# Edge softmax in steps of 512 columns, with the forward maxima of a backward step kept in PSUM

## The reference

```
h = relu(layernorm(x)); x = x + segment_sum((h * W)[src], dst)                    # layer 0
h = relu(layernorm(x)); x = x + sage(relu(sage(h)))                               # layer 1, two mean aggregations
h = relu(layernorm(x)); x = x + attention(h, edge_attr)                           # layer 2
h = relu(layernorm(x)); x = x + segment_sum(h[src] @ W.T + b, dst) / deg          # layer 3

attention: eh = edge_attr @ W_fcr.T                        # 212,500 x 64
           m  = segment_max(eh, dst);  ex = exp(eh - m[dst])
           agg = segment_sum(ex / segment_sum(ex)[dst] * ((h @ W_fc.T)[src] + eh), dst)
           h_new = relu(where(deg > 0, agg + h @ loop_W, h))
```

## Time and profile before

| stretch | us | what runs |
|---|---|---|
| 0 to 388 | 388 | keys sorted, first norm, first 64 pieces cleared; the scatter begins at 251.7 |
| 388 to 746 | 358 | forward softmax steps; scatter goes on; DMA share 0.99 |
| 746 to 905 | 159 | backward steps alone, last pieces cleared; DMA share 1.01 |
| 905 to 2462 | 1557 | backward steps with chunks 0 to 640 |
| 2462 to 2590 | 128 | last 60 chunks; the scatter ends at 2553 |
| 2590 to 6919 | 4329 | rest of layer 0, layers 1 to 3 |
| profiled execution | 6921.18 | span 6919.3, granted TensorE clock 0.913 |

### The profile page before, as it was taken

How to read it: one execution, slowest core, us unless ns; L and a number is a source line. 1 busy time by engine, 2 the same in 40 slices (tenths; PEclk the granted TensorE clock), 3 DMA queues, 4 the chain that set the end, 5 groups by cost and what they waited for, 6 DMA issues and landing times.

```text
span 6919.3 us, 127730 instructions
## 1 busy us (share of the span) xinstructions
PE 5262.2 (76%) x47666; PEld 4799.9 (69%) x47667; DVE 4606.4 (67%) x6014; ACT 3720.1 (54%) x2906; POOL 3433.8 (50%) x3412
## 2 busy tenths in 40 slices
PE   0057478888888753999999999855888888788886
PEld 0023267777777653999999999855777777677776
DVE  9757567777777658788877888733555555555554
ACT  0100167666666543788777777600555454454565
POOL 0457777777777750000000000077777777777730
PEclk9988789999999886999999999977999999999998
DMA  9999977666666545666666666533777677676785
GB/s 344 351 273 297 335 234 215 209 214 210 212 214 215 175 117 141 181 195 194 191 189 186 195 196 197 161 80 90 158 151 159 153 156 154 140 155 148 157 143 110
DMA packets 1628347, 1313.89 MB, mean 190 GB/s; under 512 B 911250, under 2 KB 1528211, under 8 KB 1627311
## 3 DMA queue, kind: packets, MB, share of 16 engines
q1 hardware_dynamic: 840725, 948.43, 46.1%
q10 hardware_dynamic: 674448, 299.80, 18.4%
q0 software_dynamic: 112592, 57.76, 5.1%
HBM read 833.34 MB, written 311.54 MB: 165 GB/s over the span
## 4 chain that ended last, share of the span: by engine, by line
PE 40%; DVE 7%; ACT 5%; issue 4%; DMA 3%; POOL 3%; DVEq 1%; SPq 0%; ACTq 0%; POOLq 0%
PE pair L1650 22%; PE pair L1769 8%; PE wide L1793 7%; ACT u L1542 3%; POOL u L1151 3%; ACT batch L1542 1%; PE wide L1832 1%; DVE u L918 1%; DMA extra<-hi_b,tsel 1%; DMA u<-zrows,stage 1%; DVEq L415 1%; DVE batch L983 1%; DMA u<-cells 1%; PE flip L1750 0%; DVE u L616 0%
## 5 line engine op out<-in xcount | busy, mean ns | idle before, releaser
L1650 PE MATMUL pair<-tab,u 128*128 128x192 bf16 (+1 forms) x29106 | 2579.5, 249 | 184.9 <-ACT u L1400 179.7
L1650 PEld LDWEIGHTS pair<-tab,u 128*128 128x128 bf16 x29106 | 2503.9, 99 | 213.3 <-ACT u L1400 183.3
L1400 ACT ACTIVATE u<-u 128x1792 bf16<-128x1792 uint8 (+1 forms) x1360 | 2269.6, 1703 | 608.4 <-PE pair L1650 347.4
L1151 POOL DMA_INDIRECT u<-zrows,stage x1664 | 1613.7, 970 | 1318.2 <-DMA zrows<-batch 782.6
L616 DVE TENSOR_REDUCE u<-u 128x1792 bf16<-128x1792 uint8 (+1 forms) x838 | 1675.1, 2021 | 662.9 <-PE pair L1650 508.4
L1116 POOL DMA_INDIRECT cells<-val,idx x1664 | 1727.9, 1038 | 755.2 <-issue 741.7
L1769 PE MATMUL pair<-u 128*128 x4880 | 939.3, 350 | 405.7 <-DVE u L918 388.9
L1769 PEld LDWEIGHTS pair<-u 128*128 128x128 f32 x4880 | 855.8, 204 | 481.6 <-issue 480.3
L1542 ACT ACTIVATE u<-u 128x1792 bf16<-128x1792 uint8 x317 | 524.7, 1684 | 320.8 <-PE wide L1793 313.1
L1609 PE MATMUL wide<-u,wbd 128*128 128x512 f32 (+1 forms) x1120 | 508.9, 588 | 179.4 <-DMA u<-in_ea 108.2
L1632 PE MATMUL flip<-ident,u 128*128 128x128 f32 x840 | 264.7, 329 | 382.9 <-DVE u L752 370.4
(11 more groups left out here) (270 smaller groups left out, 4337.4 us busy)
## 6 DMA issues: line engine op xcount, KB each, us to landing
u<-cells SPq DMA_DIRECT2D x2100, 224.0 KB, 3.1
cells<-zt SPq DMA_DIRECT2D x100, 1568.0 KB, 15.7
u<-in_ea SPq DMA_DIRECT2D x280, 384.0 KB
ex_d<-u ACTq DMA_DIRECT2D x280, 384.0 KB, 4.2
u<-ex_d SPq DMA_DIRECT2D x208, 512.0 KB
u<-gate_d SPq DMA_DIRECT2D x280, 96.1 KB
u<-gate_d ACTq DMA_DIRECT2D x280, 96.0 KB
cells<-val,idx POOLq DMA_INDIRECT x1664
```

Of the source, the lines that this page charges most:

```text
L1151: pool.indirect_dma_start(out=ring3[:, slot, k, :], out_offset=None, in_=zrows, in_offset=bass.IndirectOffsetOnAxis(ap=stage[:, st, c:c + ...
L1400: return S.activation(to, of, ACT.Copy)
L1650: mm = M(acc(p, t // 2 * 2 + b)[:, 0:width], ring[:, q % nr, (b * CK + k) * P:(b * CK + k + 1) * P], table[:, j, 0:width], start=j == 0 an ...
```

## The change

A step has four blocks of 128 columns in place of six (`BL`), so 512 columns and 210 steps over the same 107,520 columns. The result of `bwd_before` goes to a third PSUM bank, `reach`, and `bwd_scan` reads it there; `b_pm` is written first by `bwd_sub`, and the wait on the transposes (`b_full`) moves with it. Edge and gate buffers are the same four for both directions, so backward loads run up to three steps ahead in place of one. `raw0` grows from five to six buffers and `ring0` from four to five. A step has 3, 3 and 4 chunks in turn (`PACE`), ten chunks to three steps, and its work stands at spots A, B, C, D, of which B and C fall together in steps of three. 18 steps stand alone.

```
-BL = 6
+BL = 4
-STEPS = 140
+STEPS = 210
-U0, R0 = 5, 4
+U0, R0 = 6, 5
-ALONE = 12
-PER = 5
-CLEAR_FIRST, CLEAR_EVERY, CLEAR_BESIDE = 64, 10, 2
+ALONE = 18
+PACE = (3, 3, 4)
+CLEAR_FIRST, CLEAR_EVERY = 64, 15
...
-        eh = [wide[:, h * 1024:h * 1024 + SB] for h in range(2)]
+        eh, reach = [wide[:, h * 512:h * 512 + SB] for h in range(2)], wide[:, 1024:1024 + SB]
...
-                return 1 if q % PER == 1 or q % (2 * PER) == 5 else 0
+                return 1 if q % 10 in (1, 5, 8) else 0
...
-        spots0 += [(ALONE + q // PER, q % PER, q) for q in range(T2 * NC)]
+        for k in range(ALONE, STEPS + 1):
+            parts = ("A", "BC", "D") if PACE[(k - ALONE) % 3] == 3 else ("A", "B", "C", "D")
+            spots0 += [(k, part, len(spots0) - 4 * ALONE + a) for a, part in enumerate(parts)]
...
             def bwd_before(st):
-                h, b = st % 2, STEPS - 1 - st
-                dve.wait_ge(b_lg[h], 32 * (st // 2 + 1))
+                b = STEPS - 1 - st
+                dve.wait_ge(b_lg[st % 4], 32 * (st // 4 + 1))
                 dve.wait_ge(b_mm, st + 1)
-                if st >= 3:
-                    dve.wait_ge(b_full, (st - 2) * NB)
-                V.tensor_tensor_scan(b_pm[st % 3], b_gate[h][:, 0:SB], eh[h], ends[:, b:b + 1], ALU.add, ALU.max).then_inc(b_pre, 1)
+                if st:
+                    dve.wait_ge(b_scan, st)
+                V.tensor_tensor_scan(reach, gates[st % 4][:, 0:SB], eh[st % 2], ends[:, b:b + 1], ALU.add, ALU.max).then_inc(b_pre, 1)
...
-                V.tensor_tensor_scan(mx[:, ::-1], b_gate[h][:, SB:0:-1], b_pm[st % 3][:, ::-1], carry[:, :], ALU.add, ALU.max).then_inc(b_scan, 1)
+                V.tensor_tensor_scan(mx[:, ::-1], gates[st % 4][:, SB:0:-1], reach[:, ::-1], carry[:, :], ALU.add, ALU.max).then_inc(b_scan, 1)
...
             def bwd_sub(st):
+                if st >= 3:
+                    dve.wait_ge(b_full, (st - 2) * NB)
...
-                for a, b in ((0, 512), (512, SB)):
-                    mm = M(eh[h][:, a:b], wbd[:, :], edges[:, a:b], start=True, stop=True)
-                return mm
+                return M(eh[h], wbd[:, :], edges, start=True, stop=True)
```

More of the change, by code:

```diff
@@ L67 @@
 T2 = T + 2
+STEPPED = 640
 TV = 96
-ALONE = 12
-PER = 5
-CLEAR_FIRST, CLEAR_EVERY, CLEAR_BESIDE = 64, 10, 2
-LIST_ST = 80
+ALONE = 18
+PACE = (3, 3, 4)
+CLEAR_FIRST, CLEAR_EVERY = 64, 15
+LIST_ST = 120
 PARTS = tuple(itertools.pairwise((0, 25, 50, 74, T)))
@@ L80 @@
 FB = 0
-R0AT = 12 * SB * 4 + 32
-UB = R0AT + U0 * CW + 2 * R0 * CW + 544
+R0AT = 15 * SB * 4 + 32
+UB = 60736
 XW = F + 1
@@ L88 @@
 assert E <= KC * P and G * GE <= KC * P and N < PAD and KC == 1 << LK and GP <= P and TV % 2 == 0
-assert EAT[UT - 1] == T and (STEPS + 1 - ALONE) * PER <= (T + 2) * NC and STEPS % 4 == 0
+assert EAT[UT - 1] == T and STEPS % 2 == 0 and R0AT + (U0 + 2 * R0) * CW <= UB
 def gnn_kernel(nc, x, first_row, first_dst, dst_blk, dst_cols, src_cols, src_keys, dst_keys, ea2, w0, w1, b1, w2, b2, wfcr, wfc,
@@ L162, in gnn_kernel @@
         g0i, g0f = sb("g0i", [GP, GPK], i32), sb("g0f", [GP, GPK])
-        shared = sb("shared", [P, GPK * T])
-        below = shared[0:GP, :].rearrange("p (a t) -> p a t", a=GPK)
+        shared = sb("shared", [P, max(GPK * T, STEPS + 1)])
+        below = shared[0:GP, 0:GPK * T].rearrange("p (a t) -> p a t", a=GPK)
         ends = shared[:, 0:STEPS + 1]
@@ L185, in gnn_kernel @@
         unit = SB * 4
[L186 to L192, removed]
+        area = [at(FB + a * unit + a // 6 * 32, unit) for a in range(11)]
+        f_ea, f_pm, b_pm, mx, xe = area[0:4], area[6:8], area[6:9], area[9], area[10]
+        gates = [at(FB + 4 * unit + h * (unit // 2 + 4), 2 * (SB + 1), bf16) for h in range(4)]
+        exo = [at(FB + (11 + 2 * h) * unit + 32, 2 * unit).rearrange("p (h m c) -> p h m c", h=2, m=2 * BL) for h in range(2)]
         rawe = at(RING, UE * CWE, u8).rearrange("p (s e) -> p s e", s=UE)
@@ L284, in gnn_kernel @@
         f_kept = sem("f_kept")
-        b_le = [sem(f"b_le{h}") for h in range(2)]
-        b_lg = [sem(f"b_lg{h}") for h in range(2)]
+        b_le = [sem(f"b_le{h}") for h in range(4)]
+        b_lg = [sem(f"b_lg{h}") for h in range(4)]
         b_mm, b_pre, b_scan, b_carry, b_sub, b_ex, b_xe, b_full, b_free = [
@@ L338, in owner @@
                 return 1 if q % 6 == 5 else 0
-            if p == 0 and q < (STEPS - ALONE) * PER:
-                return 1 if q % PER == 1 or q % (2 * PER) == 5 else 0
+            if p == 0 and q < STEPPED:
+                return 1 if q % 10 in (1, 5, 8) else 0
             if p == 0:
@@ L387, in tail_at @@
             return tails.get(t)
-        spots0 = [(k, j, None) for k in range(ALONE) for j in range(PER)]
-        spots0 += [(ALONE + q // PER, q % PER, q) for q in range(T2 * NC)]
+        spots0 = [(k, part, None) for k in range(ALONE) for part in "ABCD"]
+        for k in range(ALONE, STEPS + 1):
+            parts = ("A", "BC", "D") if PACE[(k - ALONE) % 3] == 3 else ("A", "B", "C", "D")
+            spots0 += [(k, part, len(spots0) - 4 * ALONE + a) for a, part in enumerate(parts)]
+        assert len(spots0) - 4 * ALONE <= T2 * NC
+        spots0 += [(STEPS + 1, "", q) for q in range(len(spots0) - 4 * ALONE, T2 * NC)]
         def at0(q):
@@ L780, in _ @@
             dve.wait_ge(s_carry, 32)
-            for k, j, q in spots0:
+            for k, part, q in spots0:
                 if q == 0:
@@ L797, in _ @@
                 if k < STEPS:
-                    if j == 0:
+                    if "A" in part:
                         bwd_scan(k)
-                    elif j == 1:
+                    if "B" in part:
                         bwd_sub(k)
-                    elif j == 2 and k + 1 < STEPS:
+                    if "C" in part and k + 1 < STEPS:
                         bwd_before(k + 1)
-                    elif j == 4:
+                    if "D" in part:
                         bwd_mul(k)
@@ L1226, in bwd_edges @@
                 b = STEPS - 1 - st
[L1227 to L1231, removed]
+                sp.wait_ge(f_mm, STEPS)
+                if st >= 4:
+                    sp.wait_ge(b_mm, st - 3)
+                sp.dma_start(f_ea[st % 4], ea2[:, b * SB:(b + 1) * SB]).then_inc(b_le[st % 4], 16)
             def bwd_gates(st):
                 b = STEPS - 1 - st
-                if st >= 2:
-                    sp.wait_ge(b_scan, st - 1)
+                sp.wait_ge(f_scan, STEPS)
+                if st >= 4:
+                    sp.wait_ge(b_scan, st - 3)
                 for a in range(2):
-                    sp.dma_start(b_gate[st % 2][a * F:(a + 1) * F, :],
-                                 gate_d[a, b * SB:(b + 1) * SB + 1].partition_broadcast(F)).then_inc(b_lg[st % 2], 16)
+                    sp.dma_start(gates[st % 4][a * F:(a + 1) * F, :],
+                                 gate_d[a, b * SB:(b + 1) * SB + 1].partition_broadcast(F)).then_inc(b_lg[st % 4], 16)
             sp.wait_ge(s_prep, marks["gate"])
@@ L1249, in _ @@
                     nclear += 1
+            for st in range(3):
+                bwd_edges(st)
             for st in range(2):
                 bwd_gates(st)
-                bwd_edges(st)
-            for k, j, q in spots0:
-                if q is None and j < CLEAR_BESIDE and nclear < T2:
+            for k, part, q in spots0:
+                if q is None and part in "AC" and nclear < T2:
                     clear_next(nclear)
@@ L1268, in _ @@
                     load(0, t, c)
[L1269 to L1272, removed]
+                if "D" in part and k + 2 < STEPS:
+                    bwd_gates(k + 2)
+                if "D" in part and k + 3 < STEPS:
+                    bwd_edges(k + 3)
             assert nclear == T2
@@ L1444, in _ @@
                     conv_at(act, copied, 0, 0, t, c)
-                if j < NB and 1 <= k <= STEPS:
-                    turned_out(k - 1, j)
-                if j == 2 and k < STEPS:
+                for j, name in enumerate("AB"):
+                    if name in part and 1 <= k <= STEPS:
+                        turned_out(k - 1, j)
+                if "C" in part and k < STEPS:
                     exps(k)
@@ L1618, in bwd_features @@
             def bwd_features(st):
-                pe.wait_ge(b_le[st % 2], 16 * (st // 2 + 1))
+                pe.wait_ge(b_le[st % 4], 16 * (st // 4 + 1))
                 if st >= 2:
                     pe.wait_ge(b_xe, st - 1)
-                features(st % 2, b_ea[st % 2]).then_inc(b_mm, 1)
+                features(st % 2, f_ea[st % 4]).then_inc(b_mm, 1)
             def bwd_turns(st, j):
@@ L1684, in _ @@
             bwd_features(0)
-            for k, j, q in spots0:
-                if j == 1 and k + 1 < STEPS:
+            for k, part, q in spots0:
+                if "B" in part and k + 1 < STEPS:
                     bwd_features(k + 1)
-                if j < NB and 1 <= k <= STEPS:
-                    bwd_turns(k - 1, j)
```

(3 more changed lines are left out.)

5 lines of the change are left out of this document (2 added, 3 removed).

## The result

| kernel | median us | lowest to highest | runs |
|---|---|---|---|
| before | 6921.38 | 6916.78 to 6924.64 | 4 |
| after | 6796.24 | 6788.63 to 6800.33 | 4 |

The ratio is 0.9818, with a 95% interval of 0.9803 to 0.9834: 125 us faster. The mechanism is the one forecast, a scatter that is no longer held, but the gain is 12 us more than the sum. The profiled execution took 6794.83 us (span 6792.9), 126.4 us less span than before. In the rows of after every line number is one to five higher: the scatter is L1119, the chunks L1653, the chunk loads L1214, the backward scan L742, the forward scan of a backward step L735.

A forecast was written before the change was run, and what follows sets the result against it. POOL's layer 0 scatter, held by DVE scans reading two SBUF tensors, was taken as the bound: 6921.2 - 114 = 6807, plus 1.6 against the median of the runs, 6808 us; own range 6797 to 6825, 8-in-10 range 6797 to 6885.

The forecast's parts named there:

- The excess: Layer 0 scatter on POOL: transfer time above 0.958 us each, from scans reading two SBUF tensors; 115 us, 114 to go.
- Rival 3: Backward scan still holds POOL though one input is in PSUM; gain only 31 us, 6890 us; chance 0.06.
- rival 4: Each of 210 SBUF-to-SBUF carry copies shuts POOL out for 0.15 us; 32 us come back, 6839 us; chance 0.05.
- The queue of POOL: Layer 0 scatter: same transfers, lists and waits, so it ends near 2439, 114 us earlier, from freed transfers alone.
- Nothing behind 2590 changes but its start: Everything after layer 0's stretch, which ends near 2590, only starts earlier and keeps its length; no gain or loss there.
- Are they in time?: Layer 0 chunks: three terms put their end at 2412, 63 us before the scatter-bound 2475, so POOL still decides.
- Forward steps: Forward softmax stretch, now 210 scans of 512 columns: grows by 20 us, between 0 and 70.
- The alone steps: Softmax steps run without chunks before the first chunk load: 15 us more, between 0 and 30.
- The pace: Softmax steps with chunks in layer 0: ten chunks take 22 us where they took 24.0.
- more waiting of SP for POOL than 131.9 us: Expected sign in SP's queue of chunk loads: longer waits for POOL than before, since chunks come up to it earlier.
- Rival 1: Chunks end last: pace stays 24.0 us for ten chunks, gain of 50 us, 6871 us; chance 0.19.
- Rival 2: Each step keeps PE's 2.2 us wait for `bwd_mul`: 26.2 us for ten chunks, slower at 7012 us; chance 0.06.

## Why the prediction was right and where it fell short

**Right: what bounds the kernel, and what held it.** The excess went from 115.5 to 1.6 us, 114 less; the term was 114. The experiment with the maxima in SBUF brought it back to 85.9. That edit leaves PE's work as it is, and the time was 83 us above that of the changed kernel. (PE is the fullest engine from 905 to 2400 in the kernel before: the slices read 8 tenths, 7 at the end; the 6 to 7 given above are those of its weight loads.) Rival 3 is out. So is rival 4 with its 32 us: 210 copies together with all else left 1.6 us of excess. The seven transfers after 388 that still take over 1.01 us all start under an addition of two SBUF tensors, six under L758 and one under L703. The Trainium skill ("SBUF — State Buffer", "Who interferes with whom") says that a copy can enter a mode that takes both ports, and that GpSimd is then blocked. No run here shows that block, nor its absence: by the prediction's own formula a copy of 0.15 us that did block would lengthen a transfer by at most 0.15 + 0.77 - 0.96 = -0.04 us, which is nothing. Rival 4 should have been priced so.

**Where the sum fell short: "The queue of POOL. It has the same 1664 transfers, lists and waits".** This step put all of POOL's queue but the held transfers at no change, and it is the one that failed: with the 5 us of the next step it carried the time below the range. The scatter was to end 114 us earlier, near 2439, and ended 121.9 earlier (2552.4 to 2430.5). Beside the 114 stand 2.0 us from the eight additions to the lists in POOL's queue, 6.3 from its waits, and 0.4 against it from a later start. The additions, before and after (durations in ns):

```profile
L1091 POOL DMA_INDIRECT extra<-hi_b,tsel x24: 1541/1562/2848, 732.7 to 3698.4; - x24
```
```profile
L1094 POOL DMA_INDIRECT extra<-hi_b,tsel x24: 1541/1562/1622, 726.8 to 3578.2; - x24
```

The longest was 2848 ns and is now 1622: two of the eight started under the old scan and were held as well. I had counted the one form of POOL's transfers and not the other; that is a miss of mechanism, though a small one, and its size is chance: in the other three kernels with two SBUF inputs at steps of 768 the eight are 0, 0 and 0.3 us longer than now, as they happen to fall. Of the 6.3 us, 5.2 are the node table's wait (37.6 to 32.3). I had taken it for a constant. Over the kernels that left it in place it is 37.6, 34.2 and 33.2 with the steps of before and 31.5 to 34.5 with those of after, so most of the difference is one high value in the profile that the sum was made from. Whether a part of it belongs to the change stays open. The excess itself is 115.5, 119.5 and 122.6 in the three profiles with whole scans of 768. Each of these terms moves by some us from one execution to another, and the sum took one value of each.

**"Nothing behind 2590 changes but its start"** is 5 us off. Layer 2's gathers, before and after:

```profile
L1151 POOL DMA_INDIRECT u<-zrows,stage x1664: 938/944/1911, 4486.6 to 6634.9; - x185
```
```profile
L1154 POOL DMA_INDIRECT u<-zrows,stage x1664: 938/944/1901, 4366.9 to 6510.0; - x185
```

From first to last start these took 2148.3 us and now 2143.1. The stretch is 2148 to 2154 in the four profiles with steps of 768 and 2140 to 2145 in the six with steps of 512. The two groups do not overlap, which speaks against chance, and moving the buffers did not do it. Its cause is open. With it the account closes: 121.9 - 0.8 (a slightly longer tail behind the scatter, 37.0 us from POOL's note to the end of the chunk row instead of 36.3) + 5.3 behind layer 0 = 126.4.

**The range.** Its lower end, 6797, allowed 11 us, and only for quicker last chunks; from POOL's note to the end of the chunk row these took 37.0 us instead of 36.3, so they gave nothing. That POOL's own waits and the later layers might move by 5 us each was given no bound, in either direction.

**"Are they in time?" Right in the sum, each term off.** Forward steps were to cost +20 us and cost +45: step to step it is 403 / 210 = 1.92 us, 0.64 more than the scan, where 0.75 stood before. So most of the gap stays with each step, and the 45 lies nearer to the other end of the bound, 70. I chose by the DMA share of 0.99; it fell to 0.87, and the wait for gate loads rose from 104.5 us in 39 times to 151.8 in 75. That speaks for a wait for the landing of each load and against the bytes; no run here separates the two. The alone steps were to cost 15 and cost 18 (785.6 to 949.3, against 745.6 to 891.3). The pace was to be 22 and is 21.3. The last `bwd_mul` ends at 2339, where chunk 640 was forecast at 2334. So the pace makes good all but 5 of the 23 us lost at the start, though the loads wait 18.5 us for POOL on the way. The scan that writes PSUM takes 1286 ns on the mean of 210, the forward one that writes SBUF 1280: 0.006 us, inside the bound of 0 to 0.07.

**Wrong: "more waiting of SP for POOL than 131.9 us".** It is 89.9. The prediction's own numbers said so: the chunks would have ended at 2412 for a scatter-bound end of 2475, 63 us of room, while before it was 891 + 64 x 24.0 + 78 = 2505 for 2590, 85 us. The chunks gained less than the scatter did. The criterion that mattered, waits for POOL or none, held.

**Rival 1** was the nearest other case: the experiment with four converted chunks shows the pace of 24 and an end set by the chunks. The reason given against it, a ring of five that looses the conversion from the newest chunk, is what the runs show. **Rival 2** did not come: from 1000 to 2300 PE waits for `bwd_mul` in more steps, but 0.7 us less in each.

## What to carry to other kernels

When one engine's queue sets the end, list every instruction that stands in that queue, each form and each wait, and ask of each whether another engine holds it; then price them all, with bounds. A DVE instruction with two SBUF inputs beside a stream of POOL's indirect transfers can cost the path more than its own engine; put one input in PSUM, or leave gaps in it. And when the path is shortened, work out what was just behind it: here some two thirds of the gain were seen only with one more converted buffer (6883.0 us with four, 6800.5 with five).

## What the runs showed of the hardware that was not expected

- A held transfer needs only a moment. In the kernel with half scans one was let through in 0.04 us between two scans, and ended 0.77 us after the first. So 140 pairs of scans of 384 columns left an excess of 47.1 us, 140 scans of 768 columns one of 115.5, with the same columns and the same inputs.
- The hold bears on a transfer that starts inside the scan, and not in its first moment. In the kernel before 43 transfers began in the first 0.08 us of a scan and took their plain time; the earliest that was held began 0.083 us into it. With the maxima in SBUF one that began 0.08 us before a scan took its plain 0.95 us, and none of the 177 that began before a scan and reached into it took more than 1 us.
- The additions to the lists, which are longer transfers (1.54 us), are held like the short ones: two that started under an old scan took 2332 and 2848 ns; without such scans the longest of all takes 1622.
